# Two of the 36 samples of a deformable convolution computed from image rows on TensorE, with a gathered tile moved from the MLP into the attention

## The reference

```python
xp = x @ w_in + b_in
h = gelu(bn(depthwise_conv3x3(x)))
offset = (h @ w_off + b_off).reshape(N, H, W, GROUP, P, 2)
mask = softmax((h @ w_msk + b_msk).reshape(N, H, W, GROUP, P), axis=-1)
y = dcn_core(xp, offset, mask) @ w_out + b_out   # bilinear sample of padded xp, times mask, summed over 9
x = x + gamma1 * layer_norm(y, ln1_g, ln1_b)
m = gelu(x @ w_fc1 + b_fc1) @ w_fc2 + b_fc2
x = x + gamma2 * layer_norm(m, ln2_g, ln2_b)
t = x.reshape(8, 3136, 128)
t = t + causal_attention(ln(t), Wq, Wk, Wv)
t = t + top2_of_8_experts(ln(t), router_w, router_b, expert_w, expert_b)
```

## Time and profile before

| | |
|---|---|
| median of 3 runs | 8872.07 us (8864.89 to 8880.12) |
| the profiled execution | 8881.66 us, span 8879.9 us |
| GpSimd busy | 6554.4 us (74%) |
| VectorE busy | 5563.6 us (63%) |
| TensorE busy | 5273.8 us (59%) |
| ScalarE busy | 2767.3 us (31%) |
| DMA moved | 625.60 MB, mean 70 GB/s |
| mean granted TensorE clock | 0.78 |

### The profile page before, as it was taken

How to read it: one execution, slowest core, us unless ns; L and a number is a source line. 1 busy time by engine, 2 the same in 40 slices (tenths; PEclk the granted TensorE clock), 3 DMA queues, 4 the chain that set the end, 5 groups by cost and what they waited for, 6 DMA issues and landing times.

```text
span 8879.9 us, 85702 instructions
## 1 busy us (share of the span) xinstructions
PE 5273.8 (59%) x24752; PEld 3409.6 (38%) x24752; DVE 5563.6 (63%) x12091; ACT 2767.3 (31%) x6449; POOL 6554.4 (74%) x6898
## 2 busy tenths in 40 slices
PE   4456575555755576555665567654757556564567
PEld 2234353333533354333443344432434333342345
DVE  4666666666666666666576656765666666665554
ACT  2223232323323233322333233332323233332233
POOL 6777777777777777777777777777777777777771
PEclk7778787777877788777887788876878778776778
DMA  7333333232333323333333333333233333222220
GB/s 104 72 75 69 74 70 78 66 75 69 70 77 68 76 66 73 75 72 71 68 77 70 74 68 73 75 75 68 67 79 70 73 68 65 73 65 65 62 64 15
DMA packets 851881, 625.60 MB, mean 70 GB/s; under 512 B 551018, under 2 KB 734562, under 8 KB 851472
## 3 DMA queue, kind: packets, MB, share of 16 engines
q0 software_dynamic: 221200, 452.62, 21.0%
q1 hardware_dynamic: 629600, 167.72, 11.4%
q10 hardware_dynamic: 672, 0.24, 0.0%
HBM read 549.46 MB, written 70.57 MB: 70 GB/s over the span
## 4 chain that ended last, share of the span: by engine, by line
POOL 59%; issue 22%; PE 9%; DVE 5%; DMA 4%; SPq 1%; ACT 1%; POOLq 0%; DVEq 0%; another core or an unknown queue 0%; ACTq 0%
POOL ring L707 59%; DMA ring<-column_table,idx_r 3%; PE bank L1508 2%; PE bank L1544 2%; DVE y L1042 1%; PE bank L1517 1%; PE bank L1432 1%; PE bank L1684 1%; PE bank L1596 1%; PE bank L1661 1%; SPq L523 0%; DMA wts_r<-corner_weight 0%; SPq L493 0%; DVE ring L1032 0%; DMA tokens<-z 0%
## 5 line engine op out<-in xcount | busy, mean ns | idle before, releaser
L707 POOL DMA_INDIRECT ring<-column_table,idx_r x6860 | 6530.9, 952 | 2146.0 <-issue 2069.6
L1032 DVE TENSOR_TENSOR ring<-ring,bank 128x4608 f32<-128x4608 f32 x196 | 970.1, 4949 | 1017.7 <-POOLq L718 1016.6
L1042 DVE TENSOR_REDUCE y<-ring 128x128 f32<-128x4608 f32 x196 | 1571.1, 8016 | 16.8 <-remote 14.6
L1489 PE MATMUL bank<-ident,xn 112*128 112x112 f32 x224 | 54.9, 400 | 1722.5 <-DVE xn L968 1722.5
L1508 PE MATMUL bank<-kT,qT 128*112 128x448 f32 (+3 forms) x1792 | 824.7, 552 | 159.2 <-DVE arena L1144 152.2
L1544 PEld LDWEIGHTS bank<-v,pT 112*112 112x112 f32 x6496 | 817.7, 181 | 264.2 <-issue 186.1
L1544 PE MATMUL bank<-v,pT 112*112 112x128 f32 x6496 | 851.7, 278 | 57.1 <-DVE pT L1177 57.0
L1144 DVE TENSOR_SCALAR_CACHE_REDUCE arena<-bank 112x448 f32<-112x448 f32 x672 | 416.2, 623 | 524.6 <-PE bank L1508 495.4
L1517 PE MATMUL bank<-ident,arena 112*112 112x112 f32 x3248 | 495.6, 273 | 395.4 <-ACT arena L828 395.3
L1489 PEld LDWEIGHTS bank<-ident,xn 112*128 112x128 f32 x224 | 37.1, 217 | 1731.7 <-issue 1731.7
L1432 PE MATMUL bank<-xflat,stripes 116*128 116x448 f32 (+1 forms) x1120 | 586.9, 649 | 110.7 <-ACT xflat L790 110.6
(11 more groups left out here) (179 smaller groups left out, 7291.8 us busy)
## 6 DMA issues: line engine op xcount, KB each, us to landing
ring<-column_table,idx_r POOLq DMA_INDIRECT x6860
xflat<-dense_rows SPq DMA_DIRECT2D x56, 406.0 KB
column_table<-proj SPq DMA_DIRECT2D x196, 112.0 KB
corner_weight<-wts_s SPq DMA_DIRECT2D x56, 252.0 KB
wts_r<-corner_weight SPq DMA_DIRECT2D x196, 72.0 KB
hT<-dense_rows SPq DMA_DIRECT2D x224, 56.0 KB
tin<-tokens SPq DMA_DIRECT2D x56, 224.0 KB, 3.1
out<-xn SPq DMA_DIRECT2D x56, 224.0 KB
```

What stands on the lines that cost most here:

```text
L707: pool.indirect_dma_start(ring[:, r, e * CORNERS:(e + 1) * CORNERS, :].rearrange("p s c -> p (s c)"), None, source, bass.IndirectOffsetOnA ...
L1032: dve.tensor_tensor(corners, corners, wts_p.unsqueeze(2).broadcast_to([128, GP * CORNERS, CG]), ALU.mult)\
L1042: dve.tensor_reduce(y[:, k % BLK % 2].rearrange("p (g c) -> p g c", g=G), ring[:, bass.ds(t % RING, 1)].rearrange("p o (g e) c -> p (o g) ...
```

## The change

Two samples a token are computed from image rows, 34 are gathered (DENSE = 2). Rows are stored and loaded for both samples (twice the pieces and transfers), set_places and keep_part work for both, keep_part adding the second product to `part`. There are STAGES = 10 stages: EARLY = 2 ahead of the attention's norm being turned, and two in each q step, one at its start and one at c = j // 2. The first sample's part is kept in step q = 1, the second's where it was. set_places moves ahead of the norm. xn is turned into bank 5. The ring slots hold 136 entries instead of 144, and the sum is two instructions: three groups of 36 entries and one of 28.

The tile `between` of mlp goes. The tiles of a half slot become first, second, extra and third: 0, 1, 2, 3 where h = 0 and 4, 5, none, 6 where h = 1. extra is multiplied after q = 2's result and summed after q = 3's.

```diff
-FETCHED = GP - 1
+DENSE = 2
+FETCHED = GP - DENSE
+XN_BANK = 5
+EARLY = 2
+STAGES = DENSE * (NB // 2)
@@ timeline
-                        first, second, third, between = (
-                            ((p, n, 1), (p, n, 2), (p, n, 3), (p, n, 4)),
-                            ((p, n, 5), None, (p, n, 6), (p, n, BLK)))[h]
+                        first, second, extra, third = (
+                            ((p, n, 0), (p, n, 1), (p, n, 2), (p, n, 3)),
+                            ((p, n, 4), (p, n, 5), None, (p, n, 6)))[h]
@@ sync: store_rows, load_rows
-                    sp.dma_start(row_d[i * NJ + j].rearrange("q (t p) -> p q t", p=TT), drow[:, :, :])\
+                    sp.dma_start(row_d[i * NJ + j].rearrange("k q (t p) -> p (k q) t", p=TT),
+                                 drow.rearrange("p k q t -> p (k q) t"))\
                         .then_inc(d_rows_out, 16)
-                sp.dma_start(xflat[0:2 * PAD].rearrange("p a n -> p (a n)"),
-                             row_d[gd, 0:2].rearrange("a n -> (a n)").partition_broadcast(2 * PAD)).then_inc(d_rows_in, 16)
-                for dy in range(DY):
-                    sp.dma_start(row_wts[dy * CG:(dy + 1) * CG], row_d[gd, 2 + dy].partition_broadcast(CG))\
+                for k in range(DENSE):
+                    sp.dma_start(rows[k].rearrange("p a n -> p (a n)"),
+                                 row_d[gd, k, 0:2].rearrange("a n -> (a n)").partition_broadcast(2 * PAD))\
                         .then_inc(d_rows_in, 16)
+                    for dy in range(DY):
+                        sp.dma_start(row_wts[k][dy * CG:(dy + 1) * CG], row_d[gd, k, 2 + dy].partition_broadcast(CG))\
+                            .then_inc(d_rows_in, 16)
@@ scalar: attention
+                if now:
+                    for stage in range(EARLY):
+                        hats(gd, stage)
                 act.wait_ge(xn_turned, FIRST + g + 1)
...
                     if now:
-                        hats(gd, q)
+                        hats(gd, EARLY + 2 * q)
...
+                        if now and c == j // 2:
+                            hats(gd, EARLY + 2 * q + 1)
                     if q == 1 and second:
                         tile(*second)
-                if now:
-                    hats(gd, NT)
+                    if q == 3 and extra:
+                        tile(*extra)
@@ vector: sum_up, mlp, keep_part, attention
-                dve.tensor_reduce(
-                    y[:, k % BLK % 2].rearrange("p (g c) -> p g c", g=G),
-                    ring[:, bass.ds(t % RING, 1)].rearrange("p o (g e) c -> p (o g) c e", g=G), AX.X, ALU.add)\
+                step.did(dve.tensor_reduce(
+                    y[:, k % BLK % 2, 0:(G - 1) * CG].rearrange("p (g c) -> p g c", g=G - 1),
+                    products[:, 0:whole].rearrange("p (g e) c -> p g c e", g=G - 1), AX.X, ALU.add))
+                dve.tensor_reduce(
+                    y[:, k % BLK % 2, (G - 1) * CG:], products[:, whole:].rearrange("p e c -> p c e"), AX.X, ALU.add)\
                     .then_inc(y_made, 1)
...
-                if between:
-                    tile(*between)
                 dve.wait_ge(fc2_made, FIRST + s * 2 + half + 1)
...
+                    dve.wait_ge(d_kept, FIRST + DENSE * gd + sample)
+                    step.did(dve.tensor_tensor(row_wts[sample], bank[0][:, 0:CH], row_wts[sample], ALU.mult))
+                    step.wait()
+                    dve.tensor_tensor(part[:, f % 2], part[:, f % 2], row_wts[sample], ALU.add).then_inc(d_kept, 1)
...
                     multiply(*first)
+                if now:
+                    set_places(dense_chunk(*now)[2])
                 dve.wait_ge(tok_in[buf], (s + h) * 16)
...
                 layer_norm(tin[:, buf], xn, NT, TT, 1e-5).then_inc(xn_made, 1)
-                if now:
-                    set_places(dense_chunk(*now)[2])
...
+                        if now and q == 1 and c == 0:
+                            keep_part(*now, 0)
...
                     if second and q == 1:
                         sum_up(*second)
+                    if extra and q == 2:
+                        multiply(*extra)
+                    if extra and q == 3:
+                        sum_up(*extra)
@@ tensor: attention
                 banks_left(fronts, s * 2 + h, g)
+                if now:
+                    for stage in range(EARLY):
+                        sum_columns(di, gd, stage)
                 pe.wait_ge(xn_made, FIRST + g + 1)
...
                     if now:
-                        sum_columns(di, gd, q)
+                        sum_columns(di, gd, EARLY + 2 * q)
...
+                        if now and c == j // 2:
+                            sum_columns(di, gd, EARLY + 2 * q + 1)
```

More of the change, by code:

```diff
@@ L451, in slots @@
                             tile(p, n, k1 - 1)
-                        mlp(s, n, h, last, (p, fronts[h] + 1), g + 1 if att else 0, between, then)
+                        mlp(s, n, h, last, (p, fronts[h] + 1), g + 1 if att else 0, then)
             first_image()
@@ L621, in tile, with attention @@
                 ring_load(p, t)
-            def attention(i, j, h, s, fronts, first, second, now):
+            def attention(i, j, h, s, fronts, first, second, extra, now):
                 if first:
@@ L627, in attention, with mlp @@
                     tile(*second)
-            def mlp(s, n, half, last, fronts, n_att, between, then):
+                if extra:
+                    tile(*extra)
+            def mlp(s, n, half, last, fronts, n_att, then):
                 k0, k1 = PARTS[half]
@@ L1105, in set_places, with keep_part @@
                 step.wait()
[L1106 to L1108 removed]
+                for k in range(DENSE):
+                    dve.scalar_tensor_tensor(place[k], rows[k][:, 0], -1.0, rows[k][:, 1], ALU.max, ALU.add)\
+                        .then_inc(d_placed, 1)
+            def keep_part(p, f, sample):
                 gd = dense_chunk(p, f)[2]
[L1111 to L1115 removed]
+                dve.wait_ge(d_summed, FIRST + (DENSE * gd + sample + 1) * NB)
+                if sample == 0:
+                    if not (isinstance(p, int) and p == 0 and f < 2):
+                        dve.wait_ge(z_made, FIRST + p * PAIR_TILES + (f - 2) // 2 * BLK + (BLK if f % 2 else PARTS[0][1]))
+                    dve.tensor_tensor(part[:, f % 2], bank[0][:, 0:CH], row_wts[0], ALU.mult).then_inc(d_kept, 1)
+                else:
+                    dve.wait_ge(d_kept, FIRST + DENSE * gd + sample)
+                    step.did(dve.tensor_tensor(row_wts[sample], bank[0][:, 0:CH], row_wts[sample], ALU.mult))
+                    step.wait()
+                    dve.tensor_tensor(part[:, f % 2], part[:, f % 2], row_wts[sample], ALU.add).then_inc(d_kept, 1)
@@ L1117, in dense, with attention @@
             def dense(now):
                 set_places(dense_chunk(*now)[2])
-                keep_part(*now)
-            def attention(i, j, h, s, fronts, first, second, now):
+                for k in range(DENSE):
+                    keep_part(*now, k)
+            def attention(i, j, h, s, fronts, first, second, extra, now):
                 g = i * NJ + j
@@ L1382, in experts_front @@
                     if now:
-                        keep_part(*now)
+                        keep_part(*now, 1)
                 if ahead:
@@ L1436, in dense @@
                 i, _, gd = dense_chunk(*now)
[L1437 removed]
+                for stage in range(STAGES):
                     sum_columns(i, gd, stage)
[L1439 removed]
+                pe.wait_ge(d_kept, FIRST + DENSE * (gd + 1))
             def project(s, k):
@@ L1546, in attention @@
                         ins.then_inc(pv_made, 1)
+                        if now and c == j // 2:
+                            sum_columns(di, gd, EARLY + 2 * q + 1)
                     if q == 1 and second:
                         tile(*second)
-                if now:
-                    sum_columns(di, gd, NT)
+                    if q == 3 and extra:
+                        tile(*extra)
             def turn_x(i, c):
```

121 lines of the change are left out of this document (60 added, 61 removed).

## The result

The changed kernel takes 9068 us (median of four runs, 9035.91 to 9074.90) against 8872 for the kernel before: ratio 1.0214, 95% interval 1.0199 to 1.0229. It is slower, by 196 us. The profiled execution spans 9061.3 us. 9220 was forecast, with a range of 8700 to 9480.

What follows compares the result with a forecast made beforehand. GpSimd's gather was taken as the limit, with 16.8 us spare a half slot; terms summing to 23.8 on 137.0 over 48 half slots, plus start 418 and last stretch 1091, gave 9220 us, range 8700 to 9480.

Steps and rivals of the forecast that it cites:

- (5): Head of the attention: rows' store and load, doubled, arrive late, making the head +9 us a half slot instead of 3.5.
- rival B: Rows arrive in time, all else as forecast: 18.3 us added a half slot, time 8956 us; chance 0.27.
- The start: Before the first attention: two chunks run their sums alone, moving its beginning from 358.3 to 418 us.
- The base: Everything outside GpSimd in the kernel before needs 137.0 us of each half slot's 153.8.
- (1): MLP without the tile between its norms: gives back only 1 us a half slot, as VectorE then waits 12 to 13 for FC2.
- (2): Attention: the tile moved there from the MLP costs 8.4 us in a slot's first half, 3 otherwise; mean 5.0.
- (3): Attention's q loop: two sum_columns stages per step instead of one cost 10.1 us a half slot, bounds 7 and 13.
- (4): Head of the attention: two stages before xn is turned add 3.5 us a half slot if rows are at hand.
- (6): Attention: keep_part for the second sample, two instructions ahead of the third tile's multiply, costs 1.2 us a half slot.
- the last stretch: End of the kernel after the 48 half slots: said to take 1091 us, from 975.7 without waits for tiles.
- A: GpSimd stays the limit, additions staying below 11.4 us a half slot: 8626 us; chance 0.20.
- C: The queue costs more, head 13 and stages 13: 30.7 us added a half slot, 9550 us; chance 0.10.

Runs made afterwards that it cites:

- the kernel with narrow ones: Kernel after, each q step's second stage working on 32 of its 448 columns: 8826 us, ratio 0.9947; where the kernel before takes 14319, 14449 us, ratio 1.0091.
- the three edits together: Kernel after, one tile back between the MLP's norms, one early stage (last behind q steps), rows loaded before stripes: 14755 to 14812 us, ratios 1.0274 to 1.0322.

## Why the prediction was right, and where not

The sign, the mechanism and the range hold: the spare outside GpSimd was 16.8 us a half slot, the additions are more, and so the 246 us do not arrive. The forecast of 9220 is 152 us above the 9068 measured, and that the time still falls into the forecast's own band (9050 to 9450) is luck. Term (5), which set that band apart from rival B's, did not hold: 20.8 us were added to a half slot, where (5) made it 23.8. The start, 40 us longer than was said, lifted the time over B's upper end of 9050. Step by step:

- **The base.** 137.0 us a half slot outside GpSimd was right: the marks give 136.2. A gather still costs 1.25 us, VectorE's wait for tiles is gone, GpSimd's other waits are 500.7 us for "some 600".
- **(1) The MLP without the tile**, -1.0: measured -1.6, with a wait for FC2 of 11.8 us each time for "12 to 13". Right.
- **(2) and (3), the attention**, +5.0 and +10.1: the sum, 15.1, is the measured 14.9, but the split is most likely wrong. Four second stages come to 6.8 us by the kernel with narrow ones, of which it shows 4.7, and (3)'s lower bound was 7. (3) took the mean of all stages, 2.1 us, of which part ran at the lower clock, where in the q steps it is 1.71. Its dearer short cases are in the trace: from the first scores read to the norm of t1 the attention grew by 19.9 us with one key chunk, 17.4 with two and 11.5 to 15.4 with three and more. The other 8.1 us are the tile and whatever else grew: 7.8 at the end of the first half is in the rows (8.4 was said). For the second half 3 us were said, from one pair of attentions over seven key chunks. That pair differs by 87.2 - 82.5 = 4.7 us, so the 3 is not its reading, and seven key chunks is a case in which a tile costs little, 3.2 us for 5.2 on the mean in the kernel before. The steps show 6.9. That these are the tile's is read from the traces and was not shown by a run. If the split is as said here, two errors of about 3 us cancelled.
- **(4) The head**, +3.5 with rows at hand. Timeline of the kernel after beside rows 4; the MLP ends at 4679.65:

```profile
4684.26 0.45 DVE L1122 TENSOR_SCALAR xflat<-xflat,dcol 116x448 f32<-116x448 f32 x1
...
4688.21 3.33 PE L1467 MATMUL bank<-xflat,stripes 116*128 116x448 f32 x4 [13.89 <-ACT xflat L798]
...
4693.37 3.36 PE L1467 MATMUL bank<-xflat,stripes 116*128 116x448 f32 x4 [1.84 <-ACT xflat L798]
...
4696.52 0.95 PE L1527 MATMUL bank<-ident,xn 112*128 112x112 f32 x4
...
4703.77 0.62 DVE L1172 TENSOR_SCALAR_CACHE_REDUCE arena<-bank 112x448 f32<-112x448 f32 x1 [5.59 <-PE bank L1546]
```

The first sample's place is ready at 4685.73, +6.1 (said, for both: +6.0; both are at +6.6), the second stage ends at +17.1 (said: +16.2), the first scores are read at +24.1, 3.8 us later than before (said: 2.9 to 3.5). In the forty half slots that do not begin an image, MLP's end to first scores went from 19.3 to 23.0. Right. The stages were the longer by the clock, which the table of stretches shows (us, busy time and count of TensorE, its weight loads, VectorE, ScalarE, GpSimd, then granted clock):

```profile
4688.00:4693.00 5.00, 3.33 (x4) 1.18 (x4) 4.73 (x13) 2.13 (x4) 3.78 (x5) 0.50 0.19 52
...
4704.00:4790.00 86.00, 69.33 (x418) 49.18 (x416) 53.88 (x93) 45.06 (x101) 64.90 (x70) 0.97 0.20 55
```

TensorE had stood 13.89 us, the granted clock is 0.50 (1.2 GHz), and a stage takes 3.33 us instead of 1.71.

- **(5) The rows come too late**, 5.5 us more on every half slot. This is the step that failed, in two ways. It said that the rows can't be loaded before "their store is down". But SyncE's queue in the kernel before reads so, right behind rows 10:

```profile
4463.74 2.27 SPq L603 DMA_DIRECT2D idx_r<-corner_index  x1
...
4467.29 0.27 SPq L538 DMA_DIRECT2D xflat<-dense_rows  x1
```

The load is issued 4.2 us behind a store that takes 12.9 us to land, so it does not wait for this store. In the code the store is that of chunk 2n + LEAD + h and the load that of chunk 2n + 2 + h, six half slots older; its store was down long ago. This could have been seen ahead of the prediction. And it took the pieces of a store at 10.4 us, to be paid once more when they double, 23.3 us in all. The doubled store lands after 16.1 us on the median, where it was 12.9, so twice the pieces are 3.2 us. The same place in the kernel after:

```profile
4655.87 0.51 SPq L517 DMA_DIRECT2D dense_rows<-drow  x1
...
4656.88 5.16 SPq L614 DMA_DIRECT2D idx_r<-corner_index  x1
...
4663.32 0.81 SPq L548 DMA_DIRECT2D xflat<-dense_rows  x1
```

What is left is mostly that the rows' load is issued later: the load of indices behind the store keeps SyncE for 7.0 us on the median instead of 2.2, and the rows' load starts 9.6 us behind the store instead of 4.5. From the records of the transfers, medians over the forty half slots, the first row arrived 10.9 us after the store was issued and now 15.0, and the rows took 9.7 us and now 15.1 from first to last (said: 10.2 and 16). So behind the store the doubling costs 4.1 us, not 10.4. Nor was it nothing, as the fixed time and bytes in the Trainium skill (DMA: Bandwidth & Descriptors, section Anatomy of one DMA — SWDGE (gpsimd) path) would have it for 10.5 KB more; the page gives them for transfers that GpSimd issues, and this store is SyncE's.

The last row is there at +1.6 on the median, place needs it at +4.6: in time, which is rival B's mechanism. By the prediction's own sign, a wait of several us in most half slots, (5) is wrong: late by much are only the seven half slots that begin an image, where the stripes stand ahead (114.3 of the 130.4 us of waiting; there the head went from 24.6 us to 39.2), and nine others wait 0.1 to 4.1 us. The mean of the head is +5.4 where 9.0 was said; a term of B's kind would have been 3.5.
- **(6) keep_part and the smaller sum**, +1.2 and -0.5: from the norm of t1 to the output +2.1. Small, and low by about 1.
- **The start**: the first attention was said to begin at 418 and begins at 458.4, 100.1 us later than before instead of 60. 28.1 us of this had no term: they lie ahead of the first rows' load, in the front of the first eight chunks, whose last store is issued at 215.90 instead of 187.82. There VectorE waits for one chunk's store before it makes the next chunk's values: 47.7 us in all, where it was 28.9. Behind it two chunks run alone. For the first of them ten stages took 243.43 to 293.67, 50.2 us instead of 44.4, seven of them at the lower clock, and VectorE waited 33.4 us for its rows, where it had been 11.5. +40 us.
- **The sum**: 20.8 us a half slot for 23.8, which over 48 is 156.5 for 160.8 a half slot, -206 us; the start +40; the last stretch 1088.6 for 1091, -2. Together -168, from a span of 9227 to one of 9061.

"Attention at seven chunks about 100 us": 4686.18 to 4790.10, 103.9. Of the rivals, A (8626) is ruled out by the measurement, B was right in its mechanism for six of seven half slots and wrong in its time (8956), because half slots that begin an image and the start cost more than it had, C did not come.

What stays open: the price of the tile's place, which no run shows where the kernel before takes 8870, and whether the three edits together win there.

## What to carry to other kernels

The change took 246 us from an engine that had 16.8 us a half slot more work than the others and put 20.8 us on the others. Compare the two numbers first: above the spare, every further gather saved is worth nothing. Work put into a loop that TensorE bounds costs TensorE's time (241.6 us of busy time, 241.8 of the end, give or take 20); measured alone, at the start of a kernel, the same stage looks more than twice as dear. The price of a tile read from one pair of attentions, at seven key chunks, was low; the mean over all cases was in the same trace. Before a transfer is said to wait for another, see in the queue's rows when it is issued: a wait on a count can be for one six steps older, and a load moved ahead of a slow issue only hands the wait to the next load of that queue.

## What the runs showed of the hardware

I had not expected that a chip could need 14300 us for a kernel that takes 8870 on another. It was so in eleven of the twelve runs here, on several chips, with the kernel before beside them each time, so nothing in the variants makes it. The traces show where the time is. The same ten small steps of VectorE's reciprocal root (each waits for the count that the one before raises), in the kernel after on the chip of the first measurement:

```profile
4792.22 0.16 DVE L952 TENSOR_TENSOR nwt<-nwt 112x4 f32<-112x4 f32 x1
4792.41 0.16 DVE L954 SCALAR_TENSOR_TENSOR nwt<-nwt,seed 112x4 f32<-112x4 f32 x1
```

and in the same kernel where it takes 14625:

```profile
2845.72 0.17 DVE L952 TENSOR_TENSOR nwt<-nwt 112x4 f32<-112x4 f32 x1
2846.70 0.16 DVE L954 SCALAR_TENSOR_TENSOR nwt<-nwt,seed 112x4 f32<-112x4 f32 x1 [0.81 <-DVE nwt L952]
2848.11 0.20 DVE L956 TENSOR_TENSOR nwt<-nwt 112x4 f32<-112x4 f32 x1 [1.24 <-DVE nwt L954]
...
2850.20 0.17 DVE L960 TENSOR_SCALAR nwt<-nwt 112x4 f32<-112x4 f32 x1 [1.23 <-DVE nwt L958]
```

The instructions take what they took, the hand-off from one to the next takes up to 1.24 us instead of 0.03. Over 1575 such hand-offs of a run (seven in each of 225 reciprocal roots): 0.034 us each in the kernel before and the kernel after as first measured, whether GpSimd gathers or not. On the other chips it depends on the gathers: in the kernel after 0.38 us on the mean (172 of 694 over 1 us, longest 1.93) within 1.4 us of a gather's issue, and 0.05 (10 of 881) elsewhere. Between engines it is far more. VectorE's waits ahead of its copy of an attention's result, in the kernel after as first measured and then on the other chip ("remote" means that nothing in the trace ended the wait):

```profile
DVE t L1220 <- PE bank L1582: 228.4, 97, 7.3
```

```profile
DVE t L1220 <- remote: 1028.2, 58, 39.2
```

From the end of TensorE's product to the start of such a copy it is 0.12 us on the mean in the first. On the other chip it is 0.21 us where no gather is issued in between or just ahead (68 times) and 11.2 us where one is (96 times), at most 33 us; many of the long ones end about 7 us after the last gather of a tile. The time in which neither TensorE nor VectorE nor ScalarE works is 386 us in the kernel after as first measured and 4793 us there. GpSimd is not slower itself, and it ends up waiting too (us in total, times, longest; the kernel before with the tile moved):

```profile
POOL ring L707 <- DMA wts_r<-corner_weight: 5473.0, 160, 129.0
POOL ring L707 <- issue: 2046.2, 6695, 6.5
```

All this fits counts that arrive late while gathers are being issued; by which path is not shown. Why on some chips and not on others, no run here shows. On such a chip the balance of a kernel is another one: narrow second stages give 2.7% where the kernel before takes 8870 and 0.9% where it takes 14300. A difference of one or two per cent should not be carried from the one to the other.

SyncE, too, can be kept by issuing alone, on either kind of chip: four loads of stripes took 19.7 and 22.6 us of its queue, and what stood behind them was late by that. A store in 4-byte pieces does it to the next load: twice the pieces, and that load's issue went from 2.2 to 7.0 us.
